# Feed-forward with block-quantised activations: quantisation reordered and its rounding unit moved to ScalarE

## The reference

```python
def fp4_quant_dequant(x):                       # blocks of 16 along the last dim
    scale = max(max(abs(block)) / 6, 1e-12)
    idx = searchsorted([.25, .75, 1.25, 1.75, 2.5, 3.5, 5.], abs(block / scale))
    q = [0., .5, 1., 1.5, 2., 3., 4., 6.][idx] * sign(block) * scale
def fp4_linear(x, w):                           # x @ w.T on the quantised values
    return einsum('bsk,nk->bsn', fp4_quant_dequant(x), fp4_quant_dequant(w))
gate, up = fp4_linear(x, w_gate), fp4_linear(x, w_up)      # 128 -> 352
out = fp4_linear(silu(gate) * up, w_down)                  # 352 -> 128
```

## Time and profile before

| | |
|---|---|
| median of 3 runs | 2061.23 us (2059.76 to 2064.73) |
| the profiled execution, its time | 2063.71 us |
| its span, first to last instruction | 2061.9 us |
| first feed-forward, from its first normalisation to its last statistics | 38.78 to 211.71 us: 172.93 us |
| second feed-forward, the same | 612.47 to 788.47 us: 176.00 us |
| mean granted TensorE clock in the two | 0.80 and 0.77 of full |

### The profile page before, as it was taken

The page is one execution under the profiler, slowest core; times in us unless marked ns, Lnnn a source line. Parts: engine busy times, 40 slices in busy tenths (PEclk is TensorE's granted clock), DMA queues, the critical chain, the costliest instruction groups (busy, mean ns, idle before and its releaser), DMA issues.

```text
span 2061.9 us, 34069 instructions
## 1 busy us (share of the span) xinstructions
PE 1301.8 (63%) x10601; PEld 852.2 (41%) x10602; DVE 1045.1 (51%) x2359; ACT 642.5 (31%) x1132; POOL 526.5 (26%) x584
## 2 busy tenths in 40 slices
PE   1566367777756565008999933888887401999891
PEld 0444245445434445005555511555554400555550
DVE  5777455666636773522222255767674442222225
ACT  1222034444443221003333310555555100333330
POOL 1334111111103340472222212212210065222220
PEclk9877578989988875559999975999999555999995
DMA  8500021121200000011111156333231011111114
GB/s 235 66 0 0 16 48 33 36 44 31 38 11 0 0 0 0 30 53 32 34 36 36 35 133 103 55 52 60 45 62 23 0 40 48 35 35 36 35 36 131
DMA packets 194423, 89.80 MB, mean 44 GB/s; under 512 B 128939, under 2 KB 186676, under 8 KB 194356
## 3 DMA queue, kind: packets, MB, share of 16 engines
q1 hardware_dynamic: 185652, 71.02, 17.0%
q0 software_dynamic: 8704, 17.91, 2.4%
HBM read 28.96 MB, written 30.03 MB: 29 GB/s over the span
## 4 chain that ended last, share of the span: by engine, by line
PE 42%; DVE 11%; issue 9%; POOL 9%; DMA 7%; SPq 6%; ACT 1%; DVEq 1%; POOLq 0%; ACTq 0%
PE PS L913 13%; PE PS L939 7%; POOL slots L1127 5%; DMA qT<-qs 5%; SPq L811 4%; PE PS L580 3%; PE PS L929 3%; PE PS L501 2%; PE PS L549 2%; PE PS L307 2%; PE PS L565 2%; SPq L1282 1%; POOL ks L767 1%; PE PS L537 1%; PE PS L878 1%
## 5 line engine op out<-in xcount | busy, mean ns | idle before, releaser
L913 PE MATMUL PS<-wgu,xTs 128*128 x584 | 306.3, 608 | 25.7 <-issue 24.6
L639 ACT ACTIVATE pt<-PS 128x768 f32<-128x768 f32 (+1 forms) x256 | 234.2, 918 | 257.5 <-PE PS L501 256.2
L1020 DVE TENSOR_TENSOR pt<-pt,PS 128x512 f32<-128x512 f32 x146 | 100.5, 688 | 338.6 <-PE PS L913 305.6
L1132 POOL DMA_INDIRECT outs<-ys,xs x144 | 137.9, 957 | 418.3 <-DVE ys L1028 412.1
L720 DVE TENSOR_REDUCE m<-PS 128x4 f32<-128x1024 f32 x128 | 156.2, 1224 | 95.2 <-PE PS L501 93.9
L720 DVE TENSOR_REDUCE sg<-PS 128x6 f32<-128x768 f32 x128 | 122.1, 955 | 128.8 <-PE PS L501 127.5
L501 PE MATMUL PS<-tables 64*128 64x192 bf16 (+2 forms) x2048 | 184.6, 260 | 0.0
L965 ACT ACTIVATE pt<-PS 128x512 f32<-128x512 f32 x146 | 87.2, 597 | 294.7 <-PE PS L913 294.7
L939 PE MATMUL PS<-wdn,pt 128*128 x1152 | 163.5, 285 | 21.4 <-issue 19.6
L1127 POOL DMA_INDIRECT slots<-xr,ix x128 | 122.8, 960 | 209.8 <-DVE ix L1011 188.5
L939 PEld LDWEIGHTS PS<-wdn,pt 128*128 128x128 f32 x1152 | 139.4, 191 | 79.7 <-issue 79.6
(11 more groups left out here) (196 smaller groups left out, 2298.5 us busy)
## 6 DMA issues: line engine op xcount, KB each, us to landing
slots<-empty SPq DMA_DIRECT2D x38, 258.0 KB, 9.9
xs<-slots SPq DMA_DIRECT2D x152, 64.5 KB, 1.8
pt<-outs SPq DMA_DIRECT2D x16, 512.0 KB, 4.2
outs<-ys,xs POOLq DMA_INDIRECT x144, 2.2
wgu<-in_L_ffn_w_gate SPq DMA_DIRECT2D x1, 2048.0 KB
wgu<-in_L_ffn_w_up SPq DMA_DIRECT2D x1, 2048.0 KB
wdn<-in_L_ffn_w_down SPq DMA_DIRECT2D x8, 256.0 KB
qT<-hqT SPq DMA_DIRECT2D x128, 4.0 KB
```

What stands on the lines that cost most here:

```text
L639: s.activation(k.pt[:, a % 4, :, 0:w], k.PS[:, self.bank:self.bank + 2, 0:w], ACT.Exp, scale=self.scale).then_inc(self.s_p, 1)
L913: t.matmul(k.PS[:, 1 + 2 * p + w, :], k.xTs[:, p, :], k.wgu[:, w, ds(e, 1), :].squeeze(1), start=True, stop=True).then_inc((self.s_gate_ps ...
L1020: v.tensor_tensor(k.hs[:, p, :], k.sgs[:, p, :], k.PS[:, 2 + 2 * p, :], ALU.mult).then_inc(self.s_h, 1)
L1132: g.indirect_dma_start(k.outs, bass.IndirectOffsetOnAxis(ap=k.xs[:, u, D:D + 1].bitcast(I32), axis=0), k.ys[:, u, :], None).then_inc(self. ...
```

## The change

- The gated product of iteration z-1 becomes the last work of VectorE's step z. It is quantised in step z+1, so still with x two iterations further on. `add` in step z is for iteration z-4 instead of z-3.
- The tiles `xh`, `xn`, `mg` (now `fxh`, `fxn`, `fmg`) and the scales exist twice, for even and odd steps; the second ones lie in memory that the attention uses for `qT`.
- The rounding unit comes from the square of the value: ScalarE squares 960 columns (`squared`), and two operations of VectorE on two tensors each take the place of the mask, the maximum and the sum. The second of them is GpSimd's subtraction, which is gone there.
- GpSimd multiplies x and h by their scales in two instructions with a semaphore each.
- TensorE's step: transposes of x, gate and up, then the down product of iteration z-3, and the transposes of h (z-2) last.
- ScalarE's step: copy of x, normalisation of x for z+2, `squared` of step z+1, Silu, copies of h.
- VectorE runs `add` between the multiplied values and the two rounding operations.
- There are N + 5 steps of the written order, of which the last find work on few engines, two in each pass of the loop, four written out ahead of it and seven behind.

```diff
 vector:
+            ch.run(v.tensor_reduce(amax, blocks, AX.X, ALU.max, apply_absolute_value=True))
+            if x and self.later(z, 2):
+                eng.wait_ge(self.s_xq, x0 + z - 1)
+            if self.has(z - 4) or (h and self.run):
+                eng.wait_ge(self.s_hq, x0 + z - 3)
+            ch.run(v.tensor_scalar(scale, amax, -1.0 / 6.0, -1e-12, ALU.mult, ALU.min))
+            ch.run(v.reciprocal(inv, scale))
+            ch.run(v.tensor_scalar(inv, inv, -NUDGE, None, ALU.mult))
+            last = v.tensor_tensor(xn.rearrange("p (n k) -> p n k", k=BLK), blocks,
+                                   inv.unsqueeze(2).broadcast_to([P, n, BLK]), ALU.mult)
+            last.then_inc(self.s_xn_read, 1)
+
+        def fn(z, p):
+            if self.has(z) or self.has(z - 2):
+                quantised(z, p)
+            if self.has(z - 4):
+                self.add(eng, z - 4)
+            if self.has(z) or self.has(z - 2):
+                eng.wait_ge(self.s_sq, q0 + z + 1)
...
+                ch.run(v.scalar_tensor_tensor(xn, mg, BASE, xn, ALU.add, ALU.add))
+                v.scalar_tensor_tensor(mg, mg, BASE, xn, ALU.add, ALU.subtract).then_inc(self.s_rounded, 1)
+            if self.has(z - 1):
+                eng.wait_ge(self.s_silu, x0 + z)
+                v.tensor_tensor(k.fxh[1 - p][:, HID:k.FW].rearrange("p (a b) -> p a b", a=2), k.sg[:, :, :],
+                                k.PS[:, 2:4, 0:I0], ALU.mult).then_inc(self.s_h, 1)
 gpsimd:
+            if x:
+                if self.later(z):
+                    eng.wait_ge(self.s_xqT_ps, x0 + z)
+                dequantised(slice(0, HID), p).then_inc(self.s_xq, 1)
+            if h:
+                if self.later(z - 2):
+                    eng.wait_ge(self.s_hqT_ps, x0 + z - 2)
+                dequantised(slice(HID, k.FW), p).then_inc(self.s_hq, 1)
 tensor (order of a step: transposes of x, gate and up, down, transposes of h):
+            if down:
+                eng.wait_ge(self.s_hqT, x0 + z - 2)
+                if self.later(z - 3):
+                    eng.wait_ge(self.s_added, x0 + z - 3)
 scalar:
+        def squared(z, p):
+            if self.has(z) or self.has(z - 2):
...
+                eng.wait_ge(self.s_xn_read, q0 + z + 1)
...
+                s.activation(k.fmg[p][:, c], k.fxn[p][:, c], ACT.Square, scale=BINADE ** 0.5).then_inc(self.s_sq, 1)
...
+            squared(z + 1, 1 - p)
```

More of the change, by code:

```diff
@@ L199 @@
     N = NT // 2
-    XC, HC_, ALL = (0, 2 * D), (2 * D, 2 * D + 2 * I0), (0, 2 * D + 2 * I0)
+    STEPS, FIRST = N + 5, 4
+    HID = 2 * D
     def __init__(self, k, run):
@@ L220, in __init__, with has, later, walk @@
         self.s_added = k.sem("ffn_added")
[L222 to L228, removed]
+    def has(self, i):
+        return not isinstance(i, int) or 0 <= i < self.N
+    def later(self, i, n=1):
+        return self.run or not isinstance(i, int) or i >= n
+    def walk(self, eng, fn, ch=None, per=0):
+        for z in range(self.FIRST):
+            fn(z, z % 2)
+        passes = (self.N - 2 - self.FIRST) // 2
+        with eng.Fori(0, passes) as m:
@@ L229, in rounds @@
             if ch:
-                ch.enter(z - 3, per)
-            fn(z, True, True, True)
+                ch.enter(m, 2 * per)
+            for i in range(2):
+                fn(2 * m + (self.FIRST + i), i)
             if ch:
[L233 to L239, removed]
+                ch.leave(passes)
@@ L241, in vector @@
+        for z in range(self.FIRST + 2 * passes, self.STEPS):
+            fn(z, z % 2)
     def vector(self, eng, ch):
         k, v = self.k, self.k.nc.vector
[L243 to L250, removed]
+        x0, q0, HID = self.x0, self.q0, self.HID
@@ L251, in fn, with quantised @@
+        def quantised(z, p):
+            x, h = self.has(z), self.has(z - 2)
+            c = slice(0 if x else HID, k.FW if h else HID)
+            b = slice(c.start // BLK, c.stop // BLK)
+            n = b.stop - b.start
+            src, xn, mg, scale = k.fxh[p][:, c], k.fxn[p][:, c], k.fmg[p][:, c], k.fscale[:, p, b]
+            blocks = src.rearrange("p (n k) -> p n k", k=BLK)
+            amax, inv = k.qt["amax"][:, b], k.qt["inv"][:, b]
             if x:
                 eng.wait_ge(self.s_xn, x0 + z + 1)
-            free = (self.s_scaled, q0 + z) if not isinstance(z, int) or z or self.run else None
@@ L254, in fn @@
[L254 to L260, removed]
+            if h:
+                eng.wait_ge(self.s_h, x0 + z - 1)
+            ch.run(v.tensor_reduce(amax, blocks, AX.X, ALU.max, apply_absolute_value=True))
+            if x and self.later(z, 2):
+                eng.wait_ge(self.s_xq, x0 + z - 1)
@@ new lines, in fn @@
+        def fn(z, p):
[5 more added lines that the diff above has]
+                eng.wait_ge(self.s_sq, q0 + z + 1)
+                c = slice(0 if self.has(z) else HID, k.FW if self.has(z - 2) else HID)
+                xn, mg = k.fxn[p][:, c], k.fmg[p][:, c]
+                ch.run(v.scalar_tensor_tensor(xn, mg, BASE, xn, ALU.add, ALU.add))
[4 more added lines that the diff above has]
+                                k.PS[:, 2:4, 0:I0], ALU.mult).then_inc(self.s_h, 1)
@@ L271, in gpsimd, with dequantised, fn @@
     def gpsimd(self, eng, ch):
[L272 to L283, removed]
+        k, g = self.k, self.k.nc.gpsimd
+        x0, q0, HID = self.x0, self.q0, self.HID
+        def dequantised(c, p):
+            b = slice(c.start // BLK, c.stop // BLK)
+            mg = k.fmg[p][:, c]
+            return g.tensor_tensor(k.xhq[:, c].rearrange("p (n k) -> p n k", k=BLK), mg.rearrange("p (n k) -> p n k", k=BLK),
+                                   k.fscale[:, p, b].unsqueeze(2).broadcast_to([P, b.stop - b.start, BLK]), ALU.mult)
+        def fn(z, p):
+            x, h = self.has(z), self.has(z - 2)
+            if x or h:
+                eng.wait_ge(self.s_rounded, q0 + z + 1)
+            if x:
+                if self.later(z):
+                    eng.wait_ge(self.s_xqT_ps, x0 + z)
+                dequantised(slice(0, HID), p).then_inc(self.s_xq, 1)
+            if h:
+                if self.later(z - 2):
+                    eng.wait_ge(self.s_hqT_ps, x0 + z - 2)
+                dequantised(slice(HID, k.FW), p).then_inc(self.s_hq, 1)
+        self.walk(eng, fn)
     def tensor(self, eng):
         k, t = self.k, self.k.nc.tensor
-        x0, q0 = self.x0, self.q0
-        def fn(z, x, h, back):
-            eng.wait_ge(self.s_scaled, q0 + z + 1)
+        x0, HID = self.x0, self.HID
+        def fn(z, p):
+            x, h, down = self.has(z), self.has(z - 2), self.has(z - 3)
             if x:
+                eng.wait_ge(self.s_xq, x0 + z + 1)
+                if self.later(z):
+                    eng.wait_ge(self.s_xqT, x0 + z)
                 for j in range(2):
@@ L294, in fn @@
                 last.then_inc(self.s_xqT_ps, 1)
[L295 to L300, removed]
             if x:
                 eng.wait_ge(self.s_xqT, x0 + z + 1)
-                if not isinstance(z, int) or z or self.run:
+                if self.later(z):
                     eng.wait_ge(self.s_h, x0 + z)
@@ L318, in fn, with normalised @@
                 last.then_inc(self.s_y_ps, 1)
-        self.rounds(eng, fn)
+            if h:
+                eng.wait_ge(self.s_hq, x0 + z - 1)
+                if self.later(z - 2):
+                    eng.wait_ge(self.s_hqT, x0 + z - 2)
+                for j in range(2):
+                    for c, (o, w) in enumerate(HC):
+                        o += HID + j * I0
+                        last = t.transpose(k.PS[0:w, 5 + j, c * P:(c + 1) * P], k.xhq[:, o:o + w], k.ident[:, :])
+                last.then_inc(self.s_hqT_ps, 1)
+        self.walk(eng, fn)
     def scalar(self, eng):
         k, s = self.k, self.k.nc.scalar
-        x0, n = self.x0, self.N
-        def normalised(i):
+        x0, q0, HID = self.x0, self.q0, self.HID
+        def normalised(i, p):
             for j in range(2):
-                ins = s.activation(k.xh[:, j * D:(j + 1) * D], k.X[:, ds(2 * i + j, 1), :].squeeze(1), ACT.Identity,
+                ins = s.activation(k.fxh[p][:, j * D:(j + 1) * D], k.X[:, ds(2 * i + j, 1), :].squeeze(1), ACT.Identity,
                                    bias=k.nmr[:, ds(2 * i + j, 1)], scale=k.rstd[:, ds(2 * i + j, 1)])
@@ L1201, in __init__ @@
                   self.qt["xn"][:, 0:8 * P].rearrange("p (a g c) -> p a g c", a=2, c=32)]
+        again = [x[:, :, :].rearrange("p g t -> p (g t)").bitcast(F32) for x in self.qT]
+        self.fxh, self.fxn, self.fmg = [self.xh, again[0]], [self.qt["xn"], again[1]], [self.qt["mg"], again[2]]
         self.mh = self.hqT[:, 0, 0, 0:32].bitcast(BF16).rearrange("p (j r) -> p j r", j=2)
```

43 lines of the change are left out of this document (28 added, 15 removed).

## The result

The changed kernel took 2078.25 us in the median (2077.82 to 2079.12, 4 runs), the kernel before 2061.82 beside it. The ratio is 1.0079 with a 95% interval of 1.0062 to 1.0097: slower by 16.4 us. The forecast was 2087, its range 2066 to 2101.

What follows compares the result with a forecast made beforehand. No engine is full: TensorE, GpSimd and VectorE take turns, and the clock is lost in the turns. Steady steps +15.6 and +12.6 us, head and tail -0.9 per stage: together +26.4, median 2087 us, range 2066 to 2101.

Steps and rivals of the forecast that it cites:

- So the next R waits for all of this: R ends VectorE's rounding; next R waits for GpSimd, TensorE through down, `add`, two operations: 9.43 us at full clock.
- The sum of a full-clock step: Feed-forward loop from rounding to rounding: 0.83 + 4.88 + 0.17 + 1.19 + 2.36 = 9.43 us.
- lost in nearly every step: TensorE pauses about 3.9 us each steady step, losing the clock instead of every second step; forecast's chance 0.70.
- The price: Low clock's cost per steady step: 1.66 us on gate and up, 0.25 on transposes; step 11.34 us.
- step 6's 6.2 us of low clock: TensorE step in the kernel before, slow from 102.04 to about 108.2; 3.1 us lost by the skill's account.
- a sign to look for: Mean granted clock in the two feed-forward stages was to fall below the 0.77 and 0.80 of before.
- The rival of a clock that is never left: TensorE stays at low clock: gate and up 4.69 us, 13.2 a step, +67 in all, 2128 us; chance 0.04.
- The Square at nothing: ScalarE's Square, taken as 1.0 us, ends 5.5 us after the rounding, before `add` can start: costs nothing.
- the steady steps: Twelve steps, 3 to 15, per feed-forward stage: 134.2 us against 118.55 and 121.61, so +15.6 and +12.6.
- No second table: Against the rival that Square and Silu need different ScalarE tables, two loads a step: 2088 to 2112 us; chance 0.03.
- the tail: Stage's end after the twelve steady steps: 24.8 us against 21.94 before, +2.8.
- the head: Stage's start up to step 3's x transposes and that step: -2.6 and -1.2 us, together -3.7 with rounding.

Runs made afterwards that it cites:

- the move in the wrong direction: Changed kernel with down moved behind the h transposes, to the end of TensorE's step: 2106.56 us, ratio 1.0222 to the kernel before.
- the filled pause: Changed kernel with 15 identity products added behind the h transposes in TensorE's pause: 2031.11 us, ratio 0.9892 to the kernel before.
- the two runs with the mask: Changed kernel with mask-and-maximum rounding, GpSimd's subtraction, no Square: down ahead of gate and up, 2049.68 us; down at the head of TensorE's step, 2032.28 us.

## Why the prediction was right, point by point

**The mechanism.** "So the next R waits for all of this": shown, by the moves of `add` and of down, each of which takes the wait away and some 60 to 84 us with it by the ratios (0.9786, 0.9671 and 0.9676 against 1.0079), by the move in the wrong direction, which lengthens the full-clock step by 0.65 us for 0.7 put ahead of down, and by the filled pause, where the clock is kept and the wait stays.

**The sum of a full-clock step**, 9.43 us, measured 9.35 and 9.33 in the changed kernel, and 9.27 and 9.32 on average in the first ten steady steps of the filled one. By parts: from the rounding to the x transposes 0.76 to 0.93 us (0.83), transposes to the end of down 4.89 (4.88), from `add` to the rounding 1.02 where 1.19 was taken, two operations 2.33 (2.36). In the 1.19 the gated product came 0.09 behind the end of the statistics; the rounding operation now starts 0.08 ahead of it (151.31 against 151.39).

**The clock**, "lost in nearly every step": in every step from 4 to 15 in either stage, gate and up took 3.8 to 5.06 us. Steps average 11.15 and 11.16 us, forecast 11.34. The price, 1.91 forecast, is 1.8. The account of the Trainium skill ("TensorE: Matmul & The Clock Gate", section "HAM oscillation — how this bites in real kernels"), half of the time at the low clock, had given 3.1 us a step. Most of that gap was my input, not the account: I had put step 6's 6.2 us of low clock into every step. In the changed kernel the granted clock is 0.82 over the 132.02 us of the twelve steps, which makes some 47.5 us at the low clock, 4.3 in each of the eleven that lost it. Half of it is an estimate of 2.2 us by the page's account, against 1.8 measured: still somewhat too high. What failed is a sign to look for: the mean granted clock of the stages rose, where I had it fall. It says how long the clock was low, not whether work was done meanwhile. The rival of a clock that is never left had gate and up at 4.69 us, which no row shows; wholly at the low clock they took 5.06 here.

**The Square at nothing**: right for the steady steps, shown by its doubling. **No second table**: a stage has one table load, in its head (at 45.5 us in the first), as before, and Square and Silu share the steps behind it without another.

**Too large: all three terms, the tail most.** The forecast of 26.4 us stands against 15.4 in the profiled executions (2063.71 to 2079.12). Of the feed-forward's 14.1, the steady steps gave 13.5 and 10.5 (forecast 15.6 and 12.6), the head -4.5 and -5.0 (-3.7), the tail +0.2 and -0.5 (+2.8). So the tail is 6.0 us off in the two stages, the steady steps 4.3 and the head 2.1, all the same way: the forecast held because its range was wide enough, not because errors met. I had carried over the end that the earlier trace rows show, at the low clock, 6.47 us behind GpSimd's last values; in the changed kernel's first stage that part is

```profile
214.12 1.38 POOL L311 TENSOR_TENSOR xhq<-qT,fscale 128x704 f32<-128x704 f32 x1 [4.83 <-DVE qT L287]
...
218.05 1.61 PE L357 MATMUL PS<-wdT,hqT 128*128 128x128 f32 x12 [0.95 <-ACT hqT L417]
219.69 0.42 DVE L298 SCALAR_TENSOR_TENSOR X<-PS,X 128x256 f32<-128x256 f32 x1 [3.40 <-PE PS L357]
220.16 0.49 DVE L185 BATCH_NORM_STATS2 bn<-X 128x6 f32<-128x128 f32 x2
```

with a down product of 1.61 us, from 215.50 to 220.65 in 5.15. In the kernel before, its counterpart was

```profile
207.80 2.93 PE L316 MATMUL PS<-wdT,hqT 128*128 128x128 f32 x12 [0.95 <-ACT hqT L349]
```

The clock was back for it now, and I had kept it low. That is 1.3 of the 2.6 us by which this stage's tail was too long; the rest lies in the two steps ahead of it, 9.3 and 6.2 us where I had 10.0 and 6.8. The head gained 0.8 to 1.3 us a stage more than I had worked out; why stays open.

**The rest of the kernel**, all of the span but the two feed-forward stages, differs by 1.3 us between the two profiled executions, and that can't be told from chance: in the profiles of the ten experiments and the two kernels it is between 1704 and 1715 us.

## What to carry to other kernels

When a pipeline is deepened, write down for each wait which step of the other engine it names, and then where in that step the awaited work stands. Here a result that is four iterations old by its index was computed in the step that had just begun, and the waiter stood in front of the work that starts the next one; moving ten lines of TensorE's program turned 0.8% slower into 3% faster. A measured wait that is hidden in one order (GpSimd's subtraction, a low clock) is in the open in another, so such prices have to be read anew after each change of order.

## What the hardware showed

A pause's length alone doesn't tell whether the clock is lost. In the kernel before, pauses up to 2.04 us never cost it; in the kernel with 20 transposes or 10 products in the pause, it was lost in half of the steps with pauses of 1.4 to 1.6 us, and with 15 products and 0.3 to 0.4 us it never was. In the second stage of the kernel with 20 transposes, gate and up took 4.33 us in steps 5, 7 and 9, behind pauses of 1.53 us, and 2.63 in steps 6 and 8, behind longer ones of 1.59. What decides between, these runs don't settle.

VectorE stood while GpSimd multiplied. A product of two tensors on VectorE (128x960, one of them read as a broadcast) takes 1.16 us alone and 2.22 to 2.26 where it started during GpSimd's multiplication, in the two runs with the mask. It wasn't slowed evenly: in each of these cases it ended 1.01 or 1.02 us behind GpSimd's end. VectorE's operations with a number on 60 columns, 0.19 us alone, when they would have been through before it, ended 0.04 or 0.05 us behind it instead and took up to 1.37 us. GpSimd's own multiplication of h took 1.38 to 1.43 us against 1.38 or 1.39. Beside GpSimd's work, VectorE's block maxima (1.15 us), its reciprocal (0.53 us) and its product out of PSUM (0.88 us) kept their times.
